# A mixture-of-experts stage: scatters get slot lists of their own, and GpSimd issues the next gathers ahead of the wait for a scatter's landing

## The reference

```python
x_flat = x.reshape(-1, dim)                      # 4096 tokens, 256 wide
gate_logits = x_flat @ gate_w.T                  # 8 experts
topk_vals, topk_idx = jax.lax.top_k(gate_logits, 2)
topk_w = jax.nn.softmax(topk_vals, axis=-1)
comb = comb.at[jnp.arange(T)[:, None], topk_idx].add(topk_w)
for e in range(8):
    h = jax.nn.gelu(x_flat @ w1[e].T + b1[e], approximate=False)   # 1024 wide
    y = h @ w2[e].T + b2[e]
    out = out + comb[:, e:e + 1] * y
```

## Time and profile before

| | |
|---|---|
| median of 3 runs | 1495.16 us (1491.56 to 1496.29) |
| profiled execution | time 1490.46 us, span 1488.6 us |
| PE busy | 1214.1 us (82%), granted clock 0.912 of full speed on average |
| DVE, ACT, POOL busy | 792.0, 696.3, 548.2 us |
| expert stage, first up-projection to last down-projection | 1022.2 to 1453.8 us |

### The profile page before, as it was taken

One profiled execution on the slowest core, in us unless ns is written; L12 is line 12 of the kernel. 1 busy time (PEld: TensorE's weight loads), 2 busy tenths in 40 slices (PEclk: granted clock), 3 DMA queues, 4 the chain that ended last, 5 costly groups with the idle time before them and its releaser, 6 DMA issues. The chain is left out here.

```text
span 1488.6 us, 27970 instructions
## 1 busy us (share of the span) xinstructions
PE 1214.1 (82%) x9389; PEld 817.3 (55%) x9390; DVE 792.0 (53%) x1573; ACT 696.3 (47%) x1344; POOL 548.2 (37%) x452
## 2 busy tenths in 40 slices
PE   3989989833997798779887987345999999999993
PEld 1546756621334444433443345345888888888882
DVE  3855655445465756566657345464454454454441
ACT  3565544436578567756775743233323323323321
POOL 3977555211900280044000001002555656656641
PEclk7989999966999899989999997557999999999996
DMA  4755889824960695089209604943443443444437
GB/s 169 172 140 140 179 171 191 185 78 78 243 190 1 127 255 156 1 163 248 71 1 185 184 1 149 416 125 87 66 72 66 76 71 69 74 71 71 75 53 240
DMA packets 330185, 190.22 MB, mean 128 GB/s; under 512 B 273712, under 2 KB 310832, under 8 KB 327920
## 3 DMA queue, kind: packets, MB, share of 16 engines
q1 hardware_dynamic: 292880, 129.30, 36.4%
q0 software_dynamic: 24704, 54.34, 16.3%
q10 hardware_dynamic: 12512, 5.41, 1.4%
HBM read 64.85 MB, written 60.96 MB: 85 GB/s over the span
## 5 line engine op out<-in xcount | busy, mean ns | idle before, releaser
L2108 ACT ACTIVATE all_last_rows<-moe_hbank,moe_b1T 128x256 f32<-128x256 f32 x312 | 130.0, 471 | 287.9 <-PE moe_hbank L2019 265.4
L2019 PE MATMUL moe_hbank<-moe_rowT,l_w1T 128*128 128x256 f16 x1872 | 213.1, 274 | 26.4 <-DMA moe_rowT<-moe_ends 26.3
L2019 PEld LDWEIGHTS moe_hbank<-moe_rowT,l_w1T 128*128 x1872 | 181.4, 98 | 56.5 <-issue 34.3
L2034 PE MATMUL moe_ybank<-l_w2T,moe_shared 128*128 x1872 | 210.6, 273 | 0.0
L2034 PEld LDWEIGHTS moe_ybank<-l_w2T,moe_shared 128*128 128x128 f16 x1872 | 183.0, 98 | 21.5 <-issue 0.3
L1175 ACT ACTIVATE block_probs<-block_bank 128x1024 f32<-128x1024 f32 (+1 forms) x192 | 144.5, 808 | 74.3 <-PE block_bank L937 62.2
L2287 DVE TENSOR_SCALAR moe_shared<-all_last_rows 128x2048 f16<-128x2048 f32 x39 | 48.3, 1239 | 219.5 <-ACT all_last_rows L2108 219.5
L1948 POOL DMA_INDIRECT acc_scratch<-moe_ends,moe_which x78 | 128.1, 1643 | 54.8 <-DVE moe_ends L2302 24.7
L804 POOL COPY block_stack<-block_stack 128x512 f16<-128x512 f16 x16 | 10.6, 662 | 362.3 <-ACT block_stack L1159 362.3
L934 PE MATMUL block_bank<-block_qkT 128*128 128x512 f16 (+3 forms) x384 | 94.9, 335 | 46.1 <-issue 24.4
L300 POOL TENSOR_SCALAR front_raw<-front_raw 128x1024 f32<-128x1024 f32 x32 | 92.0, 2874 | 55.2 <-ACT conv_probs L525 54.9
(11 more groups left out here) (364 smaller groups left out, 2463.2 us busy)
## 6 DMA issues: line engine op xcount, KB each, us to landing
front_raw<-in_L_ffn_w POOLq DMA_DIRECT2D x32, 512.0 KB, 5.4
w_turned<-block_qk SPq DMA_DIRECT2D x32, 512.0 KB, 3.6
w_parts<-front_raw_hi POOLq DMA_DIRECT2D x32, 256.0 KB, 5.5
w_parts<-front_raw_lo POOLq DMA_DIRECT2D x32, 256.0 KB, 5.9
l_w1T<-w_turned SPq DMA_DIRECT2D x8, 1024.0 KB, 18.4
l_w2T<-w_turned SPq DMA_DIRECT2D x8, 1024.0 KB, 20.0
rows_scratch<-moe_ends ACTq DMA_DIRECT2D x4, 1056.0 KB, 6.8
front_shared<-in_x SPq DMA_DIRECT2D x8, 512.0 KB, 6.4
```

Source lines behind the costliest of these rows:

```text
L2019: last = pe.matmul(hbank[:, c, :], w1T[:, e, wp, k, c * P:(c + 1) * P], rowT[q][:, xp * CC + k, :], start=n == 0, stop=n == 5)
L2034: last = pe.matmul(ybank[q][:, t, :], (hid_hi, hid_lo)[hp][q][:, c, t * P:(t + 1) * P], w2T[:, e, wp, c, :], start=n == 0, stop=n == 3 * H ...
L2108: act.activation(hid[:, c, :], hbank[:, c, :], ACT.Gelu, bias=b1T[:, e, c:c + 1], scale=1.0 / (GAIN * GAIN)).then_inc(S["gelu_done"], 1)
```

## The change

Scatters no longer read `which`. Four further tiles, `whither`, hold a second copy of the same two columns of `slots`, made at the start of the step in which the scatter is issued. With that, gather(j+3) no longer writes over what a scatter in flight may still read, and the wait for `added` stands behind the gathers, just ahead of the scatter. Another wait, for the copy (`whither_set`), joins it. Counts, sizes and the other engines' programs are the same.

```diff
         which = [s.sb(f"which{i}", [P, GT], U32) for i in range(4)]
+        whither = [s.sb(f"whither{i}", [P, GT], U32) for i in range(4)]
...
                 def step(j, r):
+                    pool.tensor_copy(whither[r][:, :], slots[:, bass.ds(j * GT, GT)]).then_inc(S["whither_set"], 1)
                     if not early(j, 1):
-                        pool.wait_ge(S["added"], j * (16 * GT))
                         q = (r + 1) % 2
                         pool.wait_ge(S[f"xT{q}"], (j - 1 - q) * 16 + 32)
                         pool.wait_ge(S["weighed"], j * 3)
                     if not isinstance(j, int) or j + AHEAD < GROUPS:
                         gather(j + AHEAD, (r + AHEAD) % 4)
+                    if not early(j, 1):
+                        pool.wait_ge(S["added"], j * (16 * GT))
+                    pool.wait_ge(S["whither_set"], j + 1)
                     pool.wait_ge(S["y_done"], j + 1)
                     pool.sem_inc(S["passed"], 1)
                     for t in range(GT):
-                        pool.indirect_dma_start(acc, bass.IndirectOffsetOnAxis(ap=which[r][:, t:t + 1], axis=0),
+                        pool.indirect_dma_start(acc, bass.IndirectOffsetOnAxis(ap=whither[r][:, t:t + 1], axis=0),
                                                 y[r % 2][:, t, :], None, compute_op=ALU.add).then_inc(S["added"], 16)
```

More of the change, by code:

```diff
@@ L1809, in route_and_experts @@
                  "added_done", "sofar_done", "exp_done", "ratio_done", "weights_set", "placed", "prefix_kept", "counted", "plan", "keyed",
-                 "lane_hot", "col_hot", "col_valued", "spread", "slots_known", "which_set", "weighed",
+                 "lane_hot", "col_hot", "col_valued", "spread", "slots_known", "which_set", "whither_set", "weighed",
                  "bias_loaded", "h_full", "gelu_done", "hi_done", "lo_done", "y_full", "ysum_done", "y_done", "added", "passed",
```

## The result

| | before | after |
|---|---|---|
| median | 1495.72 us (4 runs, 1491.56 to 1497.42) | 1475.76 us (4 runs, 1472.46 to 1478.25) |
| ratio | | 0.9861, 95% interval 0.9839 to 0.9882 |
| profiled execution, span | 1488.6 us | 1471.7 us |
| up(3) to up(38) | 387.71 us | 366.84 us |
| GpSimd busy | 548.2 us | 601.9 us |

The change makes the kernel 20.0 us faster, 1.4%. The spans of the two profiled executions differ by 16.9 us only, since the expert stage began 4.2 us later in that of after (first up-projection at 1026.4, before at 1022.2), behind stages whose programs are the same; inside the stage 387.71 - 366.84 = 20.87 us are gone.

A forecast was written before the change was run, and what follows sets the result against it. GpSimd's turn, waiting for each scatter's landing before copy and gathers, was taken to stretch expert-stage periods from 10.48 to 11.07 us. 20.9 - 0.8 - 1.5 = 18.6 us gained, median 1476.6; main case 1474 to 1481, range 1471 to 1487.

The forecast's parts named there:

- The sum: Whole kernel: 20.9 less 0.8 less 1.5 gives a gain of 18.6 us, median from 1495.16 to 1476.6.
- The limit of 20.9 us: Time lost ahead of up-projections from group 3 to 38, against 35 periods of 10.48; the most that could be won.
- the loss that I left in: Early expert groups: 0.8 us stays at group 4, and 1.5, half of 2.96, at groups 4 to 7.
- the slow path of 9.56: Second gather's issue to its up-projection, seen in group 4 in place of 8.02; G would have to be 11.4.
- G: Second gather's issue, counted from the up-projection two groups before its own: 14.06 before, predicted 9.2 to 12.2, taken as 12.2.
- The worst case: Splits at +6.42 hold both copies until +10.0, so the second gather is issued at 12.18, taken as 12.2.
- The limit of 12.94: Latest issue of the second gather that still allows periods of 10.48: 20.96 - 8.02.
- the splits at +8.21: Case where VectorE's splits start 8.21 us behind the up-projection: copies at +6.0 to +7.0, second gather about +9.2 to +11.7.
- The port: Rival, 13%: VectorE's splits hold copies and first gather, G 13.5, period 10.76, gain only 10.5 us, 1485.
- The gathers did land earlier: Denies a rival, 7%: gathers issued earlier but landing no earlier, or SyncE's transposes late by as much; 1495 us.
- No transposes were late enough to matter: Denies the slower rival, 7%: transposes landing late in every group, period 11.81, kernel 25 us slower, 1520.
- The clock: TensorE's clock in the expert stage: 1.00 when busy, no share of its own, its chance within the 7%.

The follow-up runs named there:

- e5: The kernel after with a GpSimd fill of a 128 x 1024 spare tile between copies and gathers; 1477.18 us, ratio to before 0.9889.
- e7: The kernel before with a GpSimd fill of a 128 x 1024 spare tile between copy and gathers; 1521.34 us, ratio to before 1.0185.
- e1: The kernel after with the landing waited for first, as in before; second list and both copies kept. 1480.43 us on chip 7, 1497.40 on chip 13.

## Why the prediction was right, and where it wasn't

- **The sum.** Predicted was 1476.6 and a gain of 18.6; measured are 1475.76 and 20.0, and 20.87 inside the stage. The limit of 20.9 us, of which "no more than that can be won", was won whole. That the figure came out is in part luck: both kernels ran where gelus come late, and nothing in the prediction asked for that (see below).
- **The term that was mis-sized** is the loss that I left in: 0.8 for group 4 and 1.5 for groups 4 to 7. It is 0 in after (up(3) to up(7) take 41.92 = 4 x 10.48). The copies got out ahead of L2293, so the second gather of group 4 came at 11.2 in place of 12.2. By my own condition that is enough even with the slow path of 9.56 (20.8, under 20.96). And the slow transposes of the earlier trace rows did not recur: in groups 4 to 7 the last DMA packet of the second transpose ends 2.8 to 3.7 us behind its issue in after, 3.2 to 4.8 in before. Why they landed sooner no run here shows. With gathers a little later the loss is back: ahead of up(4) to up(7) it is 0.6 and 1.2 us in the two runs with only the copies early, 1.0 with the short fill.
- **G.** I took 12.2 out of 9.2 to 12.2; it is 11.2 for the gathers of groups 4 to 21. The worst case was priced, not the likeliest: whichever of copy and split comes first decides, and behind up(17) the copies started at +5.79 and +5.92, ahead of the first split at +6.41, and were done as the second began. The scatter starts at +2.8 to +3.1 up to the turn behind up(19), within my +2.5 to +3.1, and at +3.1 to +3.9 in the turns behind that. The wait for the weighing of group m is met about 2 us behind the start of up(m) (1207.35 for group 17 in before, up(17) at 1205.23), not ahead of it, as I had it; the gather that needs it comes more than two periods later.
- **The limit of 12.94 held.** In after from up(21) on the splits are late behind every second up-projection, by as much as in before. That was one of my signs of being wrong, and it costs nothing here. In the stretch of its timeline below, up(22) starts at 1253.55 and the second gather at 1265.84, so G is 12.29. It feeds up(24), which starts 8.67 behind it, at 1274.51, and 12.29 + 8.67 = 20.96 is two periods of 10.48. Only the gather of group 38 passes the limit, with G = 13.08, and up(38) is the one that comes 10.52 behind the last. Behind up(23), at 1264.03, the second pair of gelus comes at +4.93 and the split at +8.16, and TensorE still doesn't wait:

```profile
1253.55 5.40 PE L2023 MATMUL moe_hbank<-moe_rowT,l_w1T 128*128 128x256 f16 x48
...
1261.18 2.48 POOL L1922 COPY moe_which<-moe_slots 128x2 uint32 x1
1261.22 2.29 DVE L2293 SCALAR_TENSOR_TENSOR moe_shared<-all_last_rows,moe_shared 128x2048 f16<-128x2048 f32 x1
...
1265.84 0.99 POOL L1926 DMA_INDIRECT moe_ends<-rows_scratch,moe_which  x1 [0.30 <-issue]
...
1268.96 0.84 ACT L2112 ACTIVATE all_last_rows<-moe_hbank,moe_b1T 128x256 f32<-128x256 f32 x2 [2.48 <-PE moe_hbank L2023]
...
1272.19 1.23 DVE L2291 TENSOR_SCALAR moe_shared<-all_last_rows 128x2048 f16<-128x2048 f32 x1 [5.83 <-ACT all_last_rows L2112]
```

- **The reason was incomplete.** "One turn of GpSimd holds this chain" is right, and e5 against e7 shows it. But I read the splits at +8.21 as given, beside those at +6.42, and did not ask why VectorE was late. It was late because ScalarE was, and ScalarE was on time in the same kernel on another chip. With punctual gelus the old turn loses 370.27 - 366.84 = 3.4 us in the stage (the list alone; for before there is no trace with punctual gelus), not 20.9. So the gain is 20.0 us in the first comparison and 1493.40 - 1474.65 = 18.8 on chip 13, and would be some 4 to 5 on chip 7, judging by the two variants of after that ran there (1475.68 and 1474.86 against 1479.72).
- **What of the change brings it.** Not a list of its own (ratio 1.0037 on chip 13) and not a longer lead (1.0005), but that the copies leave the turn's end: with them ahead of the wait, 1476.62 on chip 3 although the landing is still waited for ahead of the gathers. Gathers that pass the wait too add at most 1 to 2 us, less than can be told here. The list alone and the early copies ran side by side only on chip 7 (1480.43 and 1475.68); on the chips with late gelus each was held against before.
- **The rivals.** The port does hold something in every turn: the first gather up to up(19) (2.38 in place of 1.0), later by turns the copies (3.5) and the second gather (2.75). But it gives nothing back that TensorE feels. The gathers did land earlier. No transposes were late enough to matter: from group 8 on the last packet of the second ends 2.5 to 3.4 us behind its issue, beside 3.14 for the one of the earlier trace rows that landed after 3.64. The clock was 1.00 in the stage, 0.73 only in the tail, as before.

## What to carry to other kernels

Find the period's condition as an inequality (here G + 8.02 below two periods) and state the slack before and after; a long wait that stays under it costs little, as the 98.3 us of e1, which lost 3.4 us at most, and a lead that is not renewed each turn only postpones the stall. A tiny copy of GpSimd (0.2 us alone) that met the splits of VectorE took up to 3.7 us here, so put it where VectorE is idle rather than shorten it. Before a late engine is taken as given, ask whether it is late in every group and on every chip: the size of this gain depended on it.

## What the hardware showed unexpectedly

**The same program is 17 us faster on one chip than on another**: 1480.43 and 1497.40 us for the list alone, at a granted clock of 1.00 from 1100 to 1400 us on both. On chips 3, 11 and 13 and in the first comparison, pairs of gelus start 0.5 to 2 us later than elsewhere in the same kernel, where GpSimd issues indirect DMAs with 0.30 between them at that time; on chip 7 the same issues do nothing to them. That the issues are the cause is argued from their times, not shown, since I ran no kernel without them; nor do I know what differs in the chips. In after the gelus are on time up to group 20, where the second gather is issued at +0.7 and the scatter 1.2 us behind its end.

**Fills by GpSimd go with a slow one-input split of VectorE**: with 128 x 1024 the first split took mostly 1.57 in place of 1.23, with 128 x 4096 up to 4.69. By the Trainium skill ("SBUF — State Buffer", section "Who interferes with whom") GpSimd and VectorE exclude each other also where VectorE runs in a two-port mode with one input. The rows fit that, but no run here shows in which mode the split ran.
